# Attention over a key memory: how the softmax weights are turned on end, who subtracts their high parts, and how the score banks are laid out

## What is computed

```python
q = hidden_states @ Wq.T + bq
scores = einsum('bshd,hmd->bshm', q, memory_keys) / sqrt(H)      # 4096 tokens x 4096 keys
probs = softmax(scores, axis=-1)
mem_out = einsum('bshm,hmd->bshd', probs, memory_values)
output = mem_out @ Wo.T + bo
```

## Time and profile before

| | |
|---|---|
| median of the runs | 715.12 us |
| the profiled execution | 713.79 us, of which the span from first to last instruction is 712.0 us |
| busy: TensorE, VectorE, ScalarE, GpSimd | 675.9, 549.5, 474.0, 121.9 us |
| maxima of the attention, first and last | 122.7 and 593.1 us |
| last matmul of the values | 620.3 us |
| mean granted TensorE clock | 0.995 |

### The profile page before, as it was taken

How to read it: one execution, slowest core, us unless ns; L and a number is a source line. 1 busy time by engine, 2 the same in 40 slices (tenths; PEclk the granted TensorE clock), 3 DMA queues, 4 the chain that set the end, 5 groups by cost and what they waited for, 6 DMA issues and landing times.

```text
span 712.0 us, 10456 instructions
## 1 busy us (share of the span) xinstructions
PE 675.9 (95%) x3521; PEld 503.8 (71%) x3536; DVE 549.5 (77%) x1176; ACT 474.0 (67%) x893; POOL 121.9 (17%) x226
## 2 busy tenths in 40 slices
PE   3898988999999999999999999999999999989997
PEld 3444444788888888888888888888888888745542
DVE  3799876877876886787688677778867875799885
ACT  3577887757666756756666675666666665478886
POOL 4755412102000200200020020002001021242200
PEclk9899999999999999999999999999999999999999
DMA  7011100000000000000000000000000000000001
GB/s 279 2 46 44 59 30 0 1 1 0 1 2 1 1 0 1 1 1 1 0 1 1 1 0 1 1 1 1 0 1 1 1 1 0 1 1 30 31 16 44
DMA packets 4327, 10.87 MB, mean 15 GB/s; under 512 B 859, under 2 KB 1459, under 8 KB 4147
## 3 DMA queue, kind: packets, MB, share of 16 engines
q1 hardware_dynamic: 3987, 10.21, 4.2%
q10 hardware_dynamic: 288, 0.01, 0.0%
HBM read 8.12 MB, written 2.10 MB: 14 GB/s over the span
## 4 chain that ended last, share of the span: by engine, by line
PE 82%; DVE 8%; issue 4%; ACT 4%; POOL 1%; DMA 0%; ACTq 0%; DVEq 0%; POOLq 0%
PE banks L1088 15%; PE banks L1111 8%; PE banks L1110 8%; PE banks L1112 8%; PE banks L1073 8%; PE banks L1074 8%; PE banks L1075 8%; PE banks L953 4%; PE banks L962 3%; DVE probs L697 3%; PE banks L969 2%; PE banks L1120 2%; PE banks L909 2%; ACT probs L435 1%; PE banks L901 1%
## 5 line engine op out<-in xcount | busy, mean ns | idle before, releaser
L542 ACT ACTIVATE p_hi<-banks 128x512 fp32r<-128x512 f32 x256 | 154.0, 602 | 134.4 <-PE banks L1088 134.2
L784 DVE TENSOR_TENSOR p_lo<-banks,p_hi 128x512 fp32r<-128x512 f32 x256 | 176.2, 689 | 82.6 <-ACT p_hi L542 80.7
L821 DVE TENSOR_REDUCE bank_max<-banks 128x1 f32<-128x512 f32 x256 | 171.0, 686 | 30.2 <-PE banks L1075 26.4
L553 ACT ACTIVATE probs<-banks,neg_max 128x512 f32<-128x512 f32 (+1 forms) x192 | 158.8, 833 | 14.7 <-DVE neg_max L842 14.7
L1088 PE MATMUL banks<-ident,probs 128*128 128x128 f32 x1024 | 153.4, 272 | 1.4 <-DVE p_lo L784 1.4
L1088 PEld LDWEIGHTS banks<-ident,probs 128*128 128x128 f32 x1024 | 126.2, 140 | 36.5 <-issue 5.1
L1110 PE MATMUL banks<-p_hi,kv_lo 128*128 128x512 f32 x256 | 120.0, 469 | 0.6 <-DVE p_lo L784 0.6
L446 ACT ACTIVATE probs<-probs 128x1024 bf16<-128x1024 bf16 x96 | 92.1, 979 | 33.1 <-DVE probs L697 24.3
L697 DVE SCALAR_TENSOR_TENSOR probs<-banks,wbc 128x1024 bf16<-128x1024 f32 x80 | 95.4, 1218 | 22.5 <-PE banks L953 19.5
L1073 PE MATMUL banks<-kv_lo,q_parts 128*128 128x512 f32 x256 | 102.6, 401 | 1.2 <-issue 1.2
L1111 PE MATMUL banks<-p_lo,kv_hi 128*128 128x512 f32 x256 | 101.4, 396 | 0.0
(11 more groups left out here) (87 smaller groups left out, 708.4 us busy)
## 6 DMA issues: line engine op xcount, KB each, us to landing
kv_stage<-in_keys_values SPq DMA_DIRECT2D x8, 512.0 KB, 3.5
out<-X SPq DMA_DIRECT2D x8, 256.0 KB, 2.0
X<-in_x SPq DMA_DIRECT2D x1, 1280.0 KB, 9.2
X<-in_x SPq DMA_DIRECT2D x3, 256.0 KB, 5.3
probs<-in_wup SPq DMA_DIRECT2D x1, 704.0 KB, 5.2
probs<-in_wdown SPq DMA_DIRECT2D x1, 704.0 KB, 6.6
sup_s<-in_shared_up SPq DMA_DIRECT2D x1, 88.0 KB
sdown_s<-in_shared_down SPq DMA_DIRECT2D x1, 88.0 KB
```

The source lines that it names most:

```text
L542: act.activation(p_hi[:, c % 4, :], TB[c % 2][:, :], ACT.Copy).then_inc(p_hi_done, 1)
L553: act.activation(probs[:, v % 2, i, first * N:(first + count) * N], score_banks(u, i)[:, first:first + count, :].rearrange("p b n -> p (b ...
L784: dve.tensor_tensor(p_lo[:, c % 4, :], TB[c % 2][:, :], p_hi[:, c % 4, :].bitcast(fp32), ALU.subtract).then_inc(p_lo_done, 1)
L821: dve.tensor_reduce(bank_max[:, i % 2, q:q + 1], score_banks(u, i)[:, q, :], AX.X, ALU.max).then_inc(bank_max_done, 1)
```

## The change

TensorE no longer transposes the weights. The keys are stored in another order, so that 32 consecutive columns of a score bank together with the same columns of the other banks make up a chunk of 128 keys. The exponentials go to `E2` (two score tiles); VectorE transposes them in place by squares of 32x32, in two instructions of 128x1024 for a score tile (`transpose_squares`). SyncE then moves the squares with SBUF-to-SBUF transfers: for each score tile 16 transfers (bank b, partition quarter i), each of 32 partitions by 512 fp32 (2 KB a partition, 64 KB in all), from quarter i of `E2` to quarter b of `probsT`. The eight of the first half wait for the first transpose, the others for the second. `probsT` holds two units.

ScalarE makes the high parts (`p_high`) from `probsT`, now two chunks in one instruction (128x1024, a pair, 128 pairs in all), and waits ahead of the first pair of a unit for all the unit's transfers. GpSimd subtracts (`p_low`, 128x1024); for two thirds of the last pairs VectorE does it. `p_hi` and `p_lo` have three places each. The two banks of the transposes go to the scores, which take six banks in turn; the maximum is taken of two banks at once. The values run 26 score slots (6.5 tiles) behind the scores. In ScalarE's list a score tile's pieces stand as: a pair, piece 0, piece 1, a pair, piece 2; in VectorE's: maximum of banks 2 and 3 of the last tile, its negative maximum, the work of a group where there is any, maximum of banks 0 and 1 of this tile, two transposes of the last tile.

The ring of `xT` and `xTb` and `wbc` of the feed-forward lie in `E2`; the query projection uses bank `OB[0]`; the first transposes and gates of the second feed-forward stand behind the last scores.

```diff
+SCORE_TILES = UNITS * GT
+LAG = 26
+SQ = 32
+QUADS = P // SQ
+SCORE_BANKS = 6
+HI_RING = 3
+VALUE_PAIRS = UNITS * KC // 2
+LAST_SCORE_SLOT = SCORE_TILES * BANKS
...
-        xT = sb("xT", [P, RING, N], fp32)
-        xTb = sb("xTb", [P, RING, N], bf16)
-        xq = xT[:, 0, :]
+        xq = sb("xq", [P, N], fp32)
+        E2 = sb("E2", [P, 2, BANKS, N], fp32)
+        xT = [xq[:, :]] + [E2[:, 0, c, :] for c in range(AHEAD)]
+        xTb = E2[:, 1, 0:2, :].bitcast(bf16).rearrange("p a n -> p (a n)").rearrange("p (r n) -> p r n", r=RING)
+        wbc = E2[:, 1, 2:4, :]
         expz = sb("expz", [P, 2, GT, E], fp32)
...
+        probsT = sb("probsT", [P, 2, GT * QUADS, KC, SQ], fp32)
...
+        p_hi = sb("p_hi", [P, HI_RING, GT * QUADS, 2 * SQ], fp32r)
+        p_lo = sb("p_lo", [P, HI_RING, GT * QUADS, 2 * SQ], fp32r)
...
+        OB = [banks[:, SCORE_BANKS + b, :] for b in range(2)]
+        up_banks = [banks[:, 0:2, :], banks[:, 2:4, :]]
+        y_bank, z_bank, gate_bank, xT_bank = banks[:, 4, :], banks[:, 5, :], OB[0], OB[1]
...
+        def score_bank(S, q):
+            return (S * BANKS + q) % SCORE_BANKS
...
+        def pair_probs(m):
+            w, c = divmod(2 * m, KC)
+            return probsT[:, w % 2, :, c:c + 2, :].rearrange("p a c q -> p a (c q)")
+        def on_vector(m):
+            return 2 * m + LAG > LAST_SCORE_SLOT and m % 3 != 0
...
+        def unit_moves(w):
+            return 16 * QUADS * QUADS * (GT // 2) * (w + 1)
...
+            for S in range(SCORE_TILES):
+                u, t = divmod(S, GT)
+                if S == 0:
+                    sp.wait_ge(z_done, GROUPS)
+                    sp.wait_ge(down_done, GROUPS * SLOTS)
+                if S == GT:
+                    sp.wait_ge(ffn_w_cast, 2)
+                if t == 0 and u >= 2:
+                    wait_split(sp, (u - 1) * KC // 2 - 1)
+                for h in range(2):
+                    sp.wait_ge(squares_done, 2 * S + h + 1)
+                    for b in (2 * h, 2 * h + 1):
+                        for i in range(QUADS):
+                            sp.dma_start(probsT[b * SQ:(b + 1) * SQ, u % 2, t * QUADS + i, :, :],
+                                         E2[i * SQ:(i + 1) * SQ, S % 2, b, :].rearrange("p (c q) -> p c q", q=SQ)
+                                         ).then_inc(moved[S % 2], 16)
...
+            def p_low(m):
+                pool.wait_ge(p_hi_done, m + 1)
+                pool.tensor_tensor(p_lo[:, m % HI_RING, :, :], pair_probs(m), p_hi[:, m % HI_RING, :, :].bitcast(fp32),
+                                   ALU.subtract).then_inc(p_lo_done, 1)
...
+                for S in range(SCORE_TILES + LAG // BANKS + 1):
+                    u, i = divmod(S, GT)
+                    for m in (2 * S - 11, 2 * S - 10):
+                        if 0 <= m < VALUE_PAIRS and not on_vector(m):
+                            p_low(m)
+                    g = u // 2
+                    if u % 2 == 0 and i == 1 and g + 1 < GROUPS:
+                        inverse_deviation(ATTENTION_LN + g + 1)
+                        normalize(ATTENTION_LN + g + 1, g + 1)
+                    if u % 2 == 0 and i == 0 and u < UNITS:
...
+            def p_high(m):
+                w, c = divmod(2 * m, KC)
+                if c == 0:
+                    act.wait_ge(moved[0], unit_moves(w))
+                    act.wait_ge(moved[1], unit_moves(w))
+                wait(act, pv_done, 2 * (m - HI_RING + 1))
+                act.activation(p_hi[:, m % HI_RING, :, :], pair_probs(m), ACT.Copy).then_inc(p_hi_done, 1)
...
+            def exponentials(S, piece):
+                u, i = divmod(S, GT)
+                first, count = EXP_PIECES[piece]
+                act.wait_ge(neg_max_done, S + 1)
+                if piece == 0:
+                    if S == 0:
+                        act.wait_ge(shared_up_done, GROUPS)
+                    if S == 1:
+                        act.wait_ge(up_done, GROUPS * SLOTS)
+                        act.wait_ge(weighted, GROUPS * SLOTS)
+                    wait(act, moved[S % 2], 16 * QUADS * QUADS * (S // 2))
+                at_bank = score_bank(S, first)
+                act.activation(
+                    E2[:, S % 2, first:first + count, :].rearrange("p b n -> p (b n)"),
+                    banks[:, at_bank:at_bank + count, :].rearrange("p b n -> p (b n)"), ACT.Exp,
+                    bias=neg_max[:, u % 4, i:i + 1], accum_out=row_sum[:, u % 4, i, piece:piece + 1]
+                ).then_inc(exp_done, 1)
...
+            def attention():
+                for S in range(SCORE_TILES + LAG // BANKS + 2):
+                    u, i = divmod(S, GT)
+                    first, second = 2 * S - 11, 2 * S - 10
+                    if 0 <= first < VALUE_PAIRS:
+                        p_high(first)
+                    if 1 <= S <= SCORE_TILES:
+                        exponentials(S - 1, 0)
+                        exponentials(S - 1, 1)
+                    if u % 2 == 1 and u < LAST and i == 0:
+                        copy_xT_for_q(u // 2 + 1)
+                    if u % 2 == 1 and u < LAST and i == 1:
+                        q_high(u // 2 + 1)
+                    if 0 <= second < VALUE_PAIRS:
+                        p_high(second)
+                    if 1 <= S <= SCORE_TILES:
+                        exponentials(S - 1, 2)
+                    if u >= 2 and i == 2:
+                        copy_oT(u - 2)
+                    if u >= 2 and u % 2 == 0 and i == 3:
+                        copy_y0(u // 2 - 1)
+                    if u >= 2 and u % 2 == 0 and i == 1:
...
+            def maximum(S, h):
+                dve.wait_ge(scores_done, S * BANKS + 2 * h + 2)
+                at_bank = score_bank(S, 2 * h)
+                dve.tensor_reduce(bank_max[:, S % 2, h:h + 1],
+                                  banks[:, at_bank:at_bank + 2, :].rearrange("p b n -> p (b n)"), AX.X, ALU.max
+                                  ).then_inc(bank_max_done, 1)
+            def negative_maximum(S):
+                u, i = divmod(S, GT)
+                dve.wait_ge(bank_max_done, 2 * S + 2)
+                dve.tensor_reduce(neg_max[:, u % 4, i:i + 1], bank_max[:, S % 2, :], AX.X, ALU.max, negate=True
+                                  ).then_inc(neg_max_done, 1)
+            def transpose_squares(S, h):
+                dve.wait_ge(exp_done, S * len(EXP_PIECES) + 2 + h)
+                part_of = E2[:, S % 2, 2 * h:2 * h + 2, :].rearrange("p b n -> p (b n)")
+                dve.transpose(part_of, part_of).then_inc(squares_done, 1)
+            def attention():
+                for S in range(SCORE_TILES + LAG // BANKS + 2):
+                    u, i = divmod(S, GT)
+                    if 1 <= S <= SCORE_TILES:
+                        maximum(S - 1, 1)
+                        negative_maximum(S - 1)
+                    if 0 <= 2 * S - 11 < VALUE_PAIRS and on_vector(2 * S - 11):
+                        p_low(2 * S - 11)
+                    if u >= 3 and u % 2 == 1 and i == 0:
+                        add_first_block((u - 3) // 2)
+                    if u >= 4 and u % 2 == 0 and i == 0:
+                        add_second_block((u - 4) // 2)
+                    if u % 2 == 0 and i == 1 and u // 2 + 1 < GROUPS:
+                        moments_of(ATTENTION_LN + u // 2 + 1, u // 2 + 1)
+                    if u % 2 == 1 and u < LAST and i == 1:
+                        q_low(u // 2 + 1)
+                    if u >= 2 and u % 2 == 0 and i == 1:
+                        merge_shifts(u // 2 - 1, (u - 2) % 4)
+                    if u >= 2 and u % 2 == 0 and i == 2:
+                        merge_shares(u // 2 - 1)
+                    if u == LAST and i in (1, 2):
+                        moments_of(SECOND_LN + i - 1, i - 1)
+                    if S < SCORE_TILES:
+                        maximum(S, 0)
+                    if S == 0:
+                        residual(GROUPS - 1, GROUPS - 1)
+                    if 1 <= S <= SCORE_TILES:
+                        transpose_squares(S - 1, 0)
+                        transpose_squares(S - 1, 1)
+                    if 0 <= 2 * S - 10 < VALUE_PAIRS and on_vector(2 * S - 10):
+                        p_low(2 * S - 10)
+                    if u == LAST + 1:
+                        if i == 0:
+                            moments_of(SECOND_LN + 2, 2)
...
-            def transpose_probs(u, v, c):
-                done = (u - 1) * KC + c
-                if u == 1 and c < 3:
-                    pe.wait_ge(exp_done, GT * len(EXP_PIECES) - 2 + c)
-                    pe.wait_ge(kv_lo_done, KV)
-                elif c in (0, 4, 8):
-                    pe.wait_ge(exp_done, u * GT * len(EXP_PIECES) - 2 + c // 4)
-                wait(pe, p_lo_done, done - 1)
-                for t in range(GT):
-                    last = pe.transpose(TB[c % 2][:, t * P:(t + 1) * P],
-                                        probs[:, (v + 1) % 2, t, c * P:(c + 1) * P], ident[:, :])
```

(29 more changed lines are left out.)

470 lines of the change are left out of this document (164 added, 306 removed).

## The result

The changed kernel takes 909.05 us (median of 4 runs, 908.70 to 910.07) against 715.49 for the kernel before, run beside it: a ratio of 1.270, with an interval from 1.267 to 1.273. The forecast was 709 and the range ended at 750.

A forecast was written before the change was run, and what follows sets the result against it. TensorE bound the old kernel; afterwards VectorE and ScalarE in turn, plus a wait for transfers each unit. Profiled 713.8 - 7.6 (attention) + 1 (behind it) = 707.2 us, with 1.3 for the median 708.5, rounded 709; range 667 to 750.

The forecast's parts named there:

- the issue's cost: On SyncE's queue, each of 16 transfers a score tile takes 0.40 us back to back, bounds 0.15 and 0.52.
- the landing: Time for a 64 KB transfer inside SBUF to arrive: taken as 1.8 us, bounds 1.0 and 3.0.
- The first rival: SyncE's queue of transfer issues is the bound: 0.47 us an issue gives 729 us, 0.52 gives 770; chance 0.23.
- 55c + 5.3: Time of a unit if SyncE's queue binds, c being the issue's cost: 31.15 us at 0.47.
- the tail: Behind the last score: transfers, high part, subtraction and 8 pairs of values, 25.2 us against 27.6 before.
- The ring: In attention, VectorE and ScalarE in turn between negative maxima: 6.31 us a score tile, against TensorE's 5.97.
- the second rival: An issue of 32 partitions costs 0.2 us or less: 26.9 us a unit, total 665 us; chance 0.17.
- The work of a group: Once in two units, extra ScalarE and VectorE work delays the score tiles: 3.4 us for two units, 1.7 a unit.
- the third rival: VectorE's fp32 transpose runs at half rate, 2.46 us: total 782 us; chance 0.07.
- GpSimd's subtractions: Two low-part subtractions of 2.35 us a score tile, 4.7 in all, covered by other engines' work.
- TensorE as the bound: Rival: the change works and TensorE stays the bound, 23.9 us a unit, about 620 us; chance 0.03.
- The wait at a unit's start: ScalarE idles 2 to 3 us once a unit, ahead of the first high part, until all 64 transfers land.

The follow-up runs named there:

- E2: Not a run but a buffer of the changed kernel: it holds the exponentials of two score tiles, which VectorE transposes in place; no measured time of its own.

## Why the prediction was wrong

**The step that failed is the issue's cost.** It took c = 0.40, with 0.15 and 0.52 as bounds; it is 0.633 (0.59 and the gap). The bounds were argued from rows that all had HBM at one end. The text looked for the difference between those and the new transfers in the partitions (88 or 128 against 32) and in the bytes queued ahead. Partitions don't matter inside SBUF (16 to 128), and an issue there takes 0.51 even with nothing ahead of it (L71). What did differ, both ends inside SBUF, it named nowhere as a condition, though it used the words for the landing. The upper bound was no bound. Nothing excluded a price outside the rows chosen, and the same timeline held dearer ones: the issues of 0.58 and 0.65 shown above, the first with the very spacing of 0.63. With that spacing as upper bound the range would have ended near 887 (worked out below) and not at 750.

**The first rival was the mechanism.** "The queue is the bound" got 0.23 and 724 to 770. With c = 0.633 its formula 55c + 5.3 gives 40.1 us a unit, but that formula holds only while 9c is below 5.3, up to c = 0.59; beyond it SyncE never stands idle and a unit is 64c = 40.5. All 63 intervals then go by 16c, 638 us, against 646.0 measured. With that, and 3.5 more for the last transfers in the tail (15c), the text's own sum would have given 887: 713.8 + (638.1 - 470.4) + 1 + 3.5 + 1.3. So this one price is 179 of the 200 us missed. Of the 202 us by which the sum of 707.2 missed the profiled execution, 183 lie between the first and the last negative maximum (646.0 against 462.8), 17 in the tail, and 1 each ahead of the attention and behind it.

**The ring** was right in its path, and its sum by some luck. With four transfers a unit takes 26.6, by the formula 26.9, and the total of 665 stands both in the second rival and on the chip, though the rival had cheap issues and this kernel has few. But two errors cancel in part. An undisturbed tile takes 6.10 us where the text has 6.31, as the chain of the kernel with four transfers shows between two negative maxima:

```profile
272.59 0.17 DVE neg_max L876
...
272.78 1.45 ACT E L603 x4
274.23 0.95 ACT p_hi L588
275.18 1.10 ACT E L603 x2
...
276.30 1.25 DVE E L883
277.55 1.12 DVE bank_max L868
...
278.69 0.04 DVE neg_max L876
```

The path is the text's, step by step. The double maximum adds 1.12 and the high part 0.95, less than each takes by itself, since the next instruction of an engine starts before the last one has ended. The work of a group, on the other side, takes 4.3 us in two units (53.1 from negative maximum to negative maximum, less 8 x 6.10), where the text has 3.4. It put the additions of blocks at nothing, and where they stand (298.44 to 305.71 us) an interval takes 7.27. By themselves, transposes of 128x1024 took 1.24 (taken as 1.23), the double maximum 1.20 (1.23), high parts 1.06 (1.05), as these groups of the changed kernel and the high part above show.

```profile
L884 DVE STREAM_TRANSPOSE E<-E 128x1024 f32<-128x1024 f32 x128 | 158.6, 1240 | 204.4 <-ACT E L604 204.4
...
L869 DVE TENSOR_REDUCE bank_max<-banks 128x1 f32<-128x1024 f32 x128 | 154.0, 1203 | 37.2 <-PE banks L1147 37.1
...
L400 POOL TENSOR_TENSOR p_lo<-probsT,p_hi 128x1024 fp32r<-128x1024 f32 x120 | 286.1, 2392 | 353.2 <-ACT p_hi L589 353.2
```

The rule of one element per cycle per lane (the Trainium skill, Vector Engine (DVE) Microarchitecture Reference, section 3.8) gave an estimate of 1.07; the measured 1.24 decides, 0.17 above it, and the third rival (2.46) falls.

**GpSimd's subtractions** took 2.39 where 2.35 stood, and were covered: GpSimd's idle time ahead of them is all spent waiting for high parts. **The landing** took 2.0 where 1.8 stood. **TensorE as the bound** (23.9 a unit, 620) came near only where the transposes were cut as well.

**The wait at a unit's start** is there, 8 us instead of 2 to 3. **The wait for a free `E2`** is missing from the text: with c = 0.40 it doesn't bind (6.4 us of issues, two tiles of room), with 0.633 it is what hands the queue's pace on to ScalarE inside a unit.

**The tail** was put at 25.2 us before the +1 and took 45.0. The transfers were in 21.9 us behind the last negative maximum (791.7) instead of 10.55: 11.4 more. The pairs behind took 23.1 instead of 14.6: TensorE had stood idle for 9.5 us, and its next six values matmuls started 0.43 apart (the first 0.59), later ones 0.24. It waited 1.6 and 0.8 us for low parts. The rest of the 8.5 was not split up.

## What to carry to other kernels

Where a change adds many small transfers, price the issue first: number of issues a step, times the spacing of back-to-back issues of the same kind (which memory at each end), against the step's time. Take that spacing from a row of exactly that kind or measure it alone; a row with another memory at one end is no bound. Where rows must do, take the dearest of the whole list for the upper bound, and not a choice from it. And plan on few, large transfers: the same bytes in 4 instead of 16 made the difference between 0.93 and 1.27 of the time before.

## What was not expected of the hardware

In the rounds of transfers alone, an issue with both ends in SBUF holds the queue for 0.59 us back to back and 0.51 alone, 0.16 to 0.18 more than with HBM at either end, and neither partitions (16 to 128) nor bytes (512 B to 4 KB a partition) change it by more than 0.02 (0.59 to 0.61). Other shapes with HBM at one end took 0.58 and 0.65, and a store right behind transfers inside SBUF 0.58 instead of 0.43. SyncE's and ScalarE's queues issue beside each other without loss (64 in 21 us). A megabyte through HBM and back takes 6.7 us with the 16 DMA engines full; in the kernel with everything by HBM they were busy for 7.8 us a megabyte (93% of a tile's 8.4).
